# First attention pass as pairs of 64-row products, with one side bank and a new order of the work

## The chip, the cores and the metric

The kernel runs on one core of a Trainium2 chip. The metric is the time of one execution on the device, in microseconds (us). The kernel before was run three times.

## The reference

A stack of six transformer layers (model width 256, 16 heads of 16, hidden width 1024) works on 4 sequences of 512 tokens, and a mixture of experts follows. All is float32 at the interface.

```python
for i in range(6):
    xn = adaln(x, cond, n1_w[i], n1_b[i])            # layer norm, scale and shift from cond
    q, k, v = split(xn @ qkv_w[i].T)                 # rope on q and k, 16 heads of 16
    x = x + softmax(q @ k.T / 4 + mask) @ v @ so_w[i].T
    xn = adaln(x, cond, n2_w[i], n2_b[i])
    # queries from xn, keys and values from ctx (512 rows)
    x = x + softmax(q @ kc.T / 4 + mask2) @ vc @ co_w[i].T
    xn = adaln(x, cond, n3_w[i], n3_b[i])
    x = x + gelu(xn @ f1_w[i].T + f1_b[i]) @ f2_w[i].T + f2_b[i]
# then: layer norm, router over 8 experts, top 2, capacity 640, gelu MLP of width 512
```

The change lies in the six layers. The experts at the end (the last 350 us or so) are not touched.

## The kernel before

**Jobs and slots.** One job is the attention of one sequence in one layer: 8 jobs a layer (4 self, 4 cross), 48 in all. Jobs overlap in a pipeline of slots: slot k runs the first pass of job k, the second pass of job k-1, the tail of job k-2 (normalise, output projection and, for a cross job, the whole feed-forward net) and the head of job k+1 (norm, query and key projections, rope, split into bf16 parts). Slots whose tail is a cross job carry the feed-forward work and are called long here; the others are short. There are 24 short slots with a tail, 24 long ones (two of which, at the end, have no first pass), and slots 0 and 1.

**The two passes.** Scores need float32 accuracy, so q and k are each split in three bf16 parts (high, mid, low), and six products of parts are summed inside one matmul by stacking them over the contraction: 96 rows and a mask row, 97 in all, in `qstack` and `kstack`. The first pass (`pass1`, L735) computes a tile of 128 queries by 512 keys into a ring of three PSUM banks `ps1`, and VectorE takes its row maximum (`maximum`, L949). The maxima are transposed and written as two more rows of `qstack` (chunk M, `shift_rows`). The second pass (`pass2`, L710) computes the transposed tile with the maximum already subtracted, 99 rows, into a ring of two banks `ps2`, and ScalarE takes the exponential (`exp`, L778) into `prob`. The value product (`pv`, L723) is float32 and runs for four heads at once, one in each 32-column strip of the array.

**Units.** A slot has 16 units. A unit has four first-pass tiles, four second-pass tiles, and the value products of the unit before. TensorE executes strictly in this order:

```python
for i in range(TT):                      # four steps of a unit
    if p1: pass1(k, u, i)
    if p2: pass2(k - 1, u, i)
    if i == PV_STEP: pv(k - 1, u - 1)    # PV_STEP = 1
    if i in CHUNK_STEPS: ...side chunks at place 2 * u + (0 or 1)
```

**Side chunks.** Everything else on TensorE is cut in chunks of one PSUM bank, placed at 32 places of the slot by a table written by hand (`CHUNK_PLACES`): HV, HQ, HK are projections for values, queries and keys; HT, T1, T2, LT are transposes; O is the output projection; F1 and F2 the feed-forward net; M the maxima. They go through two banks `side[0]` and `side[1]` in turn. A chunk may start when the chunk two before it has been read (`begin`). Readers: VectorE for T1, HQ, HK, O, F2; ScalarE for HT, LT, T2, HV, M and F1 (the Gelu, two of 256 columns a chunk).

**Other engines.** ScalarE and VectorE run their own copies of the same order, so what stands ahead of an exponential or a maximum delays it. ScalarE also copies the value products out (`copy_group`, L786, once in four units), makes the high and mid bf16 parts (`hi`, `mid`, L818 and L822) and loads the Gelu table and then the exponential table again in each half of the feed-forward net. GpSimd does the rope sums and the residuals of the split (L573 to L578). SyncE's queue writes the parts to DRAM (one DMA for queries, one for keys) and loads the stacks of the next job (13 DMAs for each half of the heads), in order, with its waits in the same queue.

Of the kernel before, what the change touches and what calls it, by code (L numbers as in the profile page):

```python
# [26 lines left out]
B, S = 4, 512  # L27
T = B * S
NE, FE, CAP = 8, 512, 640
P = 128  # L30
# [23 lines left out]


NORM_STEPS = {
    "HT": dict(stats=[0, 1, 2, 3], aggregate=4, newton=6, tiles=[6, 7, 8, 8]),
    "LT": dict(stats=[30, 31, 32, 33], aggregate=34, newton=35, tiles=[35, 35, 35, 35]),
}
GUESS_PLACES = {"HT": 2, "LT": 18}  # L60

SPLIT_PLACES = (10, 12, 16, 18)

PV_STEP = 1
LAST_COPY_STEP = 2
# [3 lines left out]
Q_PARTS = (0, 0, 0, 1, 1, 2)  # L69
K_PARTS = (0, 1, 2, 0, 1, 0)  # L70
NPROD = len(Q_PARTS)
MASK_ROW = NPROD * HD
SHIFT_ROW = MASK_ROW + 1
ROWS = SHIFT_ROW + 2
VROW = H * (HD + 1) + HD
FT = DFF // P
CHUNKS_PER_LAYER = 192
# [19 lines left out]
def is_cross(k):  # L97
    return k % NJ >= B

# [180 lines left out]
def layers(nc, a, x, mod, ident, identb, eps, maskrow, rows, acc, s_pad):  # L280
    with ExitStack() as ctx:
# [9 lines left out]
        qs = [sb(f"qstack{i}", [ROWS, H, S], BF16) for i in range(2)]  # L291
        ks = [sb(f"kstack{i}", [ROWS, H, S], BF16) for i in range(2)]
        parts = sb("parts", [P, 3, KD, S], BF16)
# [3 lines left out]
        v = [sb(f"v{b}", [P, TT, VROW]) for b in range(B)]  # L297
        xnT = sb("xnT", [P, KD, S])
        xnat = sb("xnat", [P, TT, D])
# [3 lines left out]
        hT = sb("hT", [P, FT, S // 2])  # L303

        aT = hT[:, 0:4, :].rearrange("p (k a) n -> p k (a n)", k=KD)
# [6 lines left out]
        mpart = sb("mpart", [P, 2, TT, 2, H // 2], BF16)  # L312
# [9 lines left out]
        bounce = [nc.dram_tensor(f"bounce{i}", (3, D, S), BF16, kind="Internal").ap() for i in range(2)]  # L322
# [14 lines left out]
        s_stack = [sem(f"stack_loaded{i}") for i in range(2)]  # L337
# [12 lines left out]
        s_read = [sem(f"chunk_read{i}") for i in range(2)]  # L350
# [14 lines left out]
        STACK_DMAS = 16 * (2 * NPROD + 1)  # L365

        def slot_chunks(k):
# [3 lines left out]
            ffn = tail and is_cross(k - 2)  # L371
# [5 lines left out]
            def put(*names):  # L377
                for name in names:
                    for c, at in enumerate(CHUNK_PLACES[name]):
                        plan[at].append((name, c))  # L380
# [3 lines left out]
            if p2:  # L384
                plan[SHIFT_PLACES[1]].append(("M", 1))
            if head:
                put("HT", "HQ", "HK")
            if ffn:
                put("LT")
            if p1:  # L390
                plan[SHIFT_PLACES[0]].append(("M", 0))
                put("HV")
            if ffn:
                for th in range(2):
                    plan[FFN1_PLACES[th]] += [("F1", c) for c in range(4 * th, 4 * th + 4)]
                    plan[FFN2_PLACES[th]].append(("F2", th))
# [14 lines left out]
        def wait_read(eng, place, k, what, c):  # L411
            n = number[(k, what, c)]
            eng.wait_ge(s_read[n % 2], place.at(n // 2 + 1, CHUNKS_PER_LAYER // 2))

        def bank_of(k, what, c):
            n = number[(k, what, c)]
            return side[:, n % 2, :], s_read[n % 2]
# [4 lines left out]

        def slot_of(j, n, ring):

            return (n + (j % NJ if ring == 3 else 0)) % ring

        def back_of(j, n, ring):

            return (n - 2 if j % NJ or n > 1 else n - 1) if ring == 3 else n - 1
# [18 lines left out]
        def _(sp):  # L448
# [20 lines left out]
            def shift_rows(k, j, hf):  # L469

                wait_read(sp, place, k, "M", hf)
                for r in range(2):
                    sp.dma_start(qs[j % 2][SHIFT_ROW + r:SHIFT_ROW + r + 1, 8 * hf:8 * hf + 8, :],
                                 mrow[8 * r:8 * r + 8, hf, :]).then_inc(s_mload[hf], 16)

            def write_parts(j):
                for w in range(2):
                    if j > 0 and w == 0:

                        for hf in range(2):  # L480
                            sp.wait_ge(s_stack[hf], place.jobs(j, STACK_DMAS))

                    sp.wait_ge(s_low, place.jobs(j, 2) + w + 1)
                    sp.dma_start(bounce[w].rearrange("r (t p) n -> p (r t) n", p=P),
                                 parts[:, :, :, :].rearrange("p r t n -> p (r t) n")).then_inc(s_bounce[w], 16)

            def load_stack(j, hf):
                if hf == 0:
                    for w in range(2):
                        sp.wait_ge(s_bounce[w], place.jobs(j + 1, 16))  # L490
# [3 lines left out]
                heads = slice(8 * hf, 8 * hf + 8)  # L494
                for w, (stack, order) in enumerate(((qs, Q_PARTS), (ks, K_PARTS))):
                    for r, part in enumerate(order):
# [16 lines left out]
            def slot(k, p2, p1, tail, head):  # L513
# [16 lines left out]
                if k == 0:  # L530

                    sp.wait_ge(s_init, 4)
# [5 lines left out]
                if head:  # L538
                    load_stack(k + 1, 1)
# [953 lines left out]
```

## Time and profile before

| | |
|---|---|
| median of three runs | 4598.32 us (4593.73 to 4600.26) |
| profiled execution, its own time | 4588.98 us |
| its span, first to last instruction | 4587.2 us |
| mean granted TensorE clock | 0.955 of full speed |
| TensorE matmul busy | 4168.8 us (91%) |
| VectorE busy | 2848.2 us (62%) |
| ScalarE busy | 2599.2 us (57%) |
| GpSimd busy | 828.0 us (18%) |

The matmul rows overlap, since matmuls are pipelined: one of 512 columns has a row of about 0.39 us, and the next can start 0.22 us after it. So the distance between starts tells TensorE's pace, and the busy share does not. The layers run from about 110 us to 4262 us of the span.

### The profile page before, as it was taken

Reading aid. Unit: us, or ns where it says so; the run is one execution under the profiler, and the core shown is the slowest. Engines: PE = TensorE matmul, PEld = TensorE weight load, DVE = VectorE, ACT = ScalarE, POOL = GpSimd, SP = SyncE. Lnnn points to the kernel's source line nnn. Section 1 sums busy time; section 2 is a strip of 40 time slices with the busy share of each in tenths; the row PEclk is TensorE's granted clock in tenths of the full one; section 3 lists DMA queues with packets and bytes.
Section 4 is the critical chain, followed back from the end, with each engine's and each line's share of the span. In section 5 each row is a group of like instructions: output and inputs, shape, how many; then the busy total and the mean of one; then the engine's idle time right before and its main releaser. Section 6 shows DMA issues by size and latency. Waiting matters only on the chain. (4 is left out here: it accounts for less than half of the span.)

```text
span 4587.2 us, 71696 instructions
## 1 busy us (share of the span) xinstructions
PE 4168.8 (91%) x20630; PEld 2034.7 (44%) x20630; DVE 2848.2 (62%) x5817; ACT 2599.2 (57%) x4638; POOL 828.0 (18%) x506
## 2 busy tenths in 40 slices
PE   2899999999999999999999999999999999998467
PEld 1243355543355543355543355543445543355445
DVE  3878755577755577855567855567765577851311
ACT  1466655556655556655556655556655566665212
POOL 3211211111211112211112211112211112200033
PEclk7899999999999999999999999999999999999789
DMA  5444422245332244332244332244423244320234
GB/s 151 75 97 87 84 43 43 43 91 90 79 51 43 43 91 85 79 56 43 43 91 80 77 60 46 43 90 75 82 53 53 43 101 85 80 47 12 73 98 97
DMA packets 179055, 321.11 MB, mean 70 GB/s; under 512 B 27928, under 2 KB 144288, under 8 KB 159904
## 3 DMA queue, kind: packets, MB, share of 16 engines
q1 hardware_dynamic: 171360, 306.69, 33.5%
q0 software_dynamic: 7296, 9.51, 1.2%
q8 instruction: 201, 3.29, 0.3%
q14 instruction: 198, 1.62, 0.2%
HBM read 226.63 MB, written 95.17 MB: 70 GB/s over the span
## 5 line engine op out<-in xcount | busy, mean ns | idle before, releaser
L949 DVE TENSOR_REDUCE negmax<-ps 128x1 f32<-128x512 f32 x3072 | 1979.1, 682 | 759.5 <-PE ps L735 738.9
L778 ACT ACTIVATE prob<-ps 128x512 f32<-128x512 f32 x3072 | 1718.5, 595 | 1156.1 <-PE ps L710 1123.3
L735 PE MATMUL ps<-kstack,qstack 97*128 97x512 bf16 x3072 | 1201.7, 392 | 108.2 <-DMA kstack<-maskrow 56.5
L710 PE MATMUL ps<-qstack,kstack 99*128 99x512 bf16 x3072 | 1194.8, 389 | 83.0 <-ACT prob L778 65.0
L723 PE MATMUL psv<-prob,v 128*32 128x512 f32 x6144 | 837.8, 618 | 0.7 <-ACT prob L778 0.7
L735 PEld LDWEIGHTS ps<-kstack,qstack 97*128 97x128 bf16 x3072 | 300.5, 98 | 1004.5 <-DVE negmax L949 598.6
L573 POOL TENSOR_TENSOR rot<-ropep 128x512 f32<-128x512 f32 x96 | 122.0, 1271 | 2627.5 <-DVE ropep L981 2598.0
L710 PEld LDWEIGHTS ps<-qstack,kstack 99*128 99x128 bf16 x3072 | 301.8, 98 | 645.1 <-ACT prob L778 457.5
L987 DVE TENSOR_TENSOR x<-x,side 128x512 f32<-128x512 f32 x144 | 99.0, 687 | 475.6 <-PE side L630 475.6
L689 PE MATMUL side<-anat,wf 128*128 128x256 f32 x1536 | 343.8, 382 | 1.0 <-ACT anat L808 0.9
L630 PE MATMUL side<-wf,hT 128*128 128x256 f32 x1536 | 340.3, 380 | 1.9 <-issue 1.9
L630 PEld LDWEIGHTS side<-wf,hT 128*128 128x128 f32 x1536 | 292.3, 190 | 46.9 <-issue 2.7
L689 PEld LDWEIGHTS side<-anat,wf 128*128 128x128 f32 x1536 | 290.6, 191 | 45.2 <-issue 5.6
L578 POOL TENSOR_TENSOR parts<-rot,parts 128x1024 bf16<-128x1024 f32 x96 | 204.1, 2126 | 324.0 <-ACT parts L822 324.0
L576 POOL TENSOR_TENSOR rot<-rot,parts 128x1024 f32<-128x1024 f32 x96 | 204.8, 2133 | 272.8 <-ACT parts L818 272.8
L723 PEld LDWEIGHTS psv<-prob,v 128*32 128x32 f32 x6144 | 121.9, 109 | 264.8 <-issue 188.5
L850 ACT ACTIVATE hT<-side,f1b 128x256 f32<-128x256 f32 x384 | 160.9, 470 | 131.5 <-PE side L689 130.9
L622 PE MATMUL side<-xnT,wself 128*128 128x512 f32 x384 | 182.8, 600 | 1.1 <-ACT xnT L808 0.9
L616 PE MATMUL side<-ident,xnat 128*128 128x128 f32 x576 | 106.2, 316 | 67.8 <-DVE xnat L941 67.8
L941 DVE TENSOR_SCALAR xnat<-x,mv,y 128x256 f32<-128x256 f32 x288 | 153.1, 566 | 2.6
L980 DVE TENSOR_TENSOR ropep<-side,cos 128x512 f32<-128x512 f32 x96 | 66.4, 692 | 116.6 <-PE side L622 113.9
L786 ACT ACTIVATE osum<-psv 128x512 f32<-128x512 f32 x192 | 114.4, 596 | 41.9 <-PE psv L723 41.9
(154 smaller groups left out, 3486.2 us busy)
## 6 DMA issues: line engine op xcount, KB each, us to landing
bounce<-parts SPq DMA_DIRECT2D x96, 768.0 KB, 3.7
qstack<-bounce SPq DMA_DIRECT2D x576, 128.0 KB
kstack<-bounce SPq DMA_DIRECT2D x576, 128.0 KB
ctxT<-in_ctxT SPq DMA_DIRECT2D x24, 512.0 KB, 5.5
nw<-in_nwT SPq DMA_DIRECT2D x18, 512.0 KB, 11.3
w<-in_w SPq DMA_DIRECT2D x16, 512.0 KB, 4.9
wself<-in_wself SPq DMA_DIRECT2D x24, 256.0 KB, 5.0
wcross<-in_wcross SPq DMA_DIRECT2D x24, 256.0 KB, 4.2
```

What stands on the lines that cost most here:

```text
L576: nc.gpsimd.tensor_tensor(rot[:, :, :], rot[:, :, :], parts[:, 0, :, :], ALU.subtract).then_inc(s_r1, 1)
L578: nc.gpsimd.tensor_tensor(parts[:, 2, :, :], rot[:, :, :], parts[:, 1, :, :], ALU.subtract).then_inc(s_low, 1)
L622: mm = nc.tensor.matmul(bank, w[:, k, m * P:(m + 1) * P], act_T[:, k, :], start=(k == 0), stop=(k == KD - 1))
L630: mm = nc.tensor.matmul(bank[:, i * D:(i + 1) * D], act_T[:, k, t * P:(t + 1) * P], w[:, k, :], start=(k == 0), stop=(k == nk - 1))
L689: mm = nc.tensor.matmul(bank[:, i * D:(i + 1) * D], wf1[:, kk, f * P:(f + 1) * P], nT[:, kk, th * (S // 2):(th + 1) * (S // 2)], start=(kk ...
L710: nc.tensor.matmul(ps2[:, slot_of(j, n, RING2), :], kk[:, h, kt * P:(kt + 1) * P], q[:, h, :], start=True, stop=True).then_inc(s_p2full, 1)
L723: mm = nc.tensor.matmul(psv[32 * i:32 * i + 32, 0, :], v[j % B][:, kt, (HD + 1) * h:(HD + 1) * h + 32], prob[:, 4 * (u % 2) + i, :], start ...
L735: nc.tensor.matmul(ps1[:, slot_of(j, n, RING1), :], q[0:SHIFT_ROW, h, t * P:(t + 1) * P], kk[0:SHIFT_ROW, h, :], start=True, stop=True).th ...
L778: nc.scalar.activation(prob[:, 4 * (u % 2) + i, :], ps2[:, slot_of(j, n, RING2), :], ACT.Exp, scale=HD ** -0.5).then_inc(s_prob, 1)
L850: ins = nc.scalar.activation(hT[:, f, :], bank[:, i * D:(i + 1) * D], ACT.Gelu, bias=f1b[:, f:f + 1])
L941: ins = nc.vector.tensor_scalar(xnat[:, t, :], x[:, TT * (j % B) + t, :], mv[:, t, 0:1], y0[:, t:t + 1], ALU.subtract, ALU.mult)
L949: nc.vector.tensor_reduce(negmax[:, h // 8, t, h % 8:h % 8 + 1], ps1[:, slot_of(j, n, RING1), :], AX, ALU.max, negate=True).then_inc(s_p1f ...
```

## The change

1. The six part products are split in two blocks of three (48 rows each). A first-pass product now contracts 49 rows (three of the part products and the mask), and heads h and h+8 have theirs in different halves of the partitions, so that the two run on two 64-row tiles of the array at once, into two banks. The first pass is 32 pairs in place of 64 products, and one VectorE instruction takes the maxima of two banks.
2. `ps1` has four banks (two pairs). The side chunks have one bank in place of two.
3. The order of a unit is written anew: one second-pass product, two pairs of the first pass, the value products, second-pass product, side chunk, second-pass product, side chunk, second-pass product.
4. F1 is read by VectorE (bias only), and Gelu is one ScalarE instruction of 2048 columns over SBUF for each half. F2 is four chunks, not two. Long and short slots have their own tables of places.
5. Each of the twelve blocks of parts is written to DRAM by its own DMA, and the stacks are loaded by 10 DMAs for each half of the heads.

```diff
-RING1 = 3
 RING2 = 2
-CHUNK_STEPS = (0, 2)
-CHUNK_PLACES = {
-    "HV": [1, 3], "T1": [4, 5, 6, 7], "HT": [5, 6], "HQ": [7, 8], "HK": [10, 11],
-    "T2": [11, 12], "O": [13, 14], "LT": [19, 20],
+PAIRS = 32
+SHORT_PLACES = {
+    "HV": [1, 3], "T1": [2, 4, 5, 7], "HT": [6, 8], "HQ": [9, 10], "HK": [12, 14],
+    "T2": [15, 17], "O": [19, 21],
 }
-SHIFT_PLACES = (20, 4)
-FFN1_PLACES = (22, 28)
-FFN2_PLACES = (25, 31)
+LONG_PLACES = {
+    "HV": [1, 3], "T1": [2, 4, 5, 7], "HT": [6, 8], "T2": [9, 10], "O": [11, 12], "HQ": [13, 14],
+    "HK": [15, 16], "LT": [17, 18], "F1": [19, 20, 21, 22, 23, 24, 25, 26], "F2": [27, 28, 30, 31],
 }
+SHORT_SHIFT, LONG_SHIFT = (23, 0), (29, 0)
...
-SPLIT_PLACES = (10, 12, 16, 18)
+SHORT_SPLIT = (13, 15, 18, 20)
+LONG_SPLIT = (16, 18, 20, 22)
+GELU_PLACES = (23, 27)
...
-Q_PARTS = (0, 0, 0, 1, 1, 2)
-K_PARTS = (0, 1, 2, 0, 1, 0)
+Q_PARTS = (0, 0, 1, 0, 1, 2)
+K_PARTS = (0, 1, 0, 2, 1, 0)
...
-        ps1 = psum("ps1", RING1)
+        ps1 = psum("ps1", 4)
...
-        side = psum("side", 2)
+        side = psum("side", 1)
...
             def begin(k, what, c):
                 n = number[(k, what, c)]
-                if n >= 2:
-                    pe.wait_ge(s_read[n % 2], place.at(n // 2, CHUNKS_PER_LAYER // 2))
-                return side[:, n % 2, :]
+                if n >= 1:
+                    pe.wait_ge(s_read, place.at(n, CHUNKS_PER_LAYER))
+                return side[:, 0, :]
...
+            def pass1(j, n):
+                m, t = divmod(n, TT)
+                if n % 16 == 0:
+                    pe.wait_ge(s_first[n // 16], place.jobs(j + 1, FIRST_DMAS))
+                if j > 0 or n >= 2:
+                    pe.wait_ge(s_p1free, place.jobs(j, PAIRS) + n - 1)
+                for e in range(2):
+                    rows = slice(first_rows(e), first_rows(e) + FIRST_ROWS)
+                    mm = nc.tensor.matmul(ps1[:, 2 * (n % 2) + e, :], qs[j % 2][rows, 8 * e + m, t * P:(t + 1) * P],
+                                          ks[j % 2][rows, 8 * e + m, :], start=True, stop=True)
+                mm.then_inc(s_p1full, 1)
...
             def slot(k, p2, p1, tail, head):
                 for u in range(SLOT_UNITS):
...
+                    if p2:
+                        pass2(k - 1, u, 0)
+                    if p1:
+                        pass1(k, 2 * u)
+                        pass1(k, 2 * u + 1)
+                    if u and p2:
+                        pv(k - 1, u - 1)
...
+                    if p2:
+                        pass2(k - 1, u, 1)
+                    for what, c in plan[2 * u]:
+                        side_work(k, what, c)
+                    if p2:
+                        pass2(k - 1, u, 2)
+                    for what, c in plan[2 * u + 1]:
+                        side_work(k, what, c)
+                    if p2:
+                        pass2(k - 1, u, 3)
...
+            def gelu(k, th):
+                wait_read(act, place, k, "F1", 4 * th + 3)
+                nc.scalar.activation(hT[th][:, :, :], hT[th][:, :, :], ACT.Gelu).then_inc(s_gelu, 1)
+                act.preload_act_table_set(EXP_SET)
...
# ScalarE, in each half unit: exponentials 0 and 1 (or 2), copy_group, side chunk, guess, hi or mid, gelu, then exponential 3
+                    if p2:
+                        for i in ((0, 1), (2,))[half]:
                             exp(k - 1, u, i)
...
+                    if ffn and at in GELU_PLACES:
+                        gelu(k, GELU_PLACES.index(at))
+                    if half == 1 and p2:
+                        exp(k - 1, u, 3)
...
# VectorE, in each half unit: one maximum of two banks, side chunk, steps of the norm
-                nc.vector.tensor_reduce(negmax[:, h // 8, t, h % 8:h % 8 + 1], ps1[:, slot_of(j, n, RING1), :], AX, ALU.max,
+                nc.vector.tensor_reduce(out_at, ps1[:, 2 * (n % 2):2 * (n % 2) + 2, :], AX, ALU.max,
                                         negate=True).then_inc(s_p1free, 1)
...
+                elif what == "F1":
+                    th, cc = divmod(c, 4)
+                    for i in range(2):
+                        f = 2 * cc + i
+                        ins = nc.vector.tensor_scalar(hT[th][:, f, :], bank[:, i * D:(i + 1) * D], f1b[:, f:f + 1], None, ALU.add)
+                    ins.then_inc(s_read, 1)
```

## Rows read from the trace of the kernel before

**Rows 1.** The page: busy time, share of the span, instructions.

```profile
span 4587.2 us, 71696 instructions
PE 4168.8 (91%) x20630; PEld 2034.7 (44%) x20630; DVE 2848.2 (62%) x5817; ACT 2599.2 (57%) x4638; POOL 828.0 (18%) x506
```

**Rows 2.** Groups by line: xcount, busy us, mean ns, idle before and releasers.

```profile
L949 DVE TENSOR_REDUCE negmax<-ps 128x1 f32<-128x512 f32 x3072 | 1979.1, 682 | 759.5 <-PE ps L735 738.9 <-issue 14.2
L778 ACT ACTIVATE prob<-ps 128x512 f32<-128x512 f32 x3072 | 1718.5, 595 | 1156.1 <-PE ps L710 1123.3 <-issue 5.2 <-PE psv L723 4.8
L818 ACT ACTIVATE parts<-rot 128x1024 bf16<-128x1024 f32 x96 | 101.0, 1052 | 49.5 <-POOL rot L574 36.7 <-DMA bounce<-parts 12.8
...
L968 DVE TENSOR_TENSOR anat<-side,recip 128x256 f32<-128x256 f32 x192 | 81.4, 424 | 6.6
L808 ACT ACTIVATE xnT<-side,mod 128x512 f32<-128x512 f32 x96 | 74.6, 777 | 38.5 <-PE side L616 37.2
L980 DVE TENSOR_TENSOR ropep<-side,cos 128x512 f32<-128x512 f32 x96 | 66.4, 692 | 116.6 <-PE side L622 113.9 <-POOL rot L574 2.7
L850 ACT ACT_TABLE_LOAD x48 | 61.6, 1283 | 0.8
```

**Rows 3.** Windows of three short and two long slots; the last pair is DMA.

```profile
core 0: us, PE busy (x) PEld busy (x) DVE busy (x) ACT busy (x) POOL busy (x), PEclk, DMA share, GB/s
1134.05:1201.78 67.73, 66.21 (x345) 26.39 (x345) 53.95 (x108) 46.26 (x84) 13.51 (x8) 1.00 0.44 79
1826.28:1893.81 67.53, 66.30 (x346) 26.37 (x345) 53.79 (x107) 46.20 (x84) 13.52 (x8) 1.00 0.45 80
3829.01:3895.70 66.69, 65.87 (x344) 25.77 (x344) 52.16 (x102) 44.70 (x81) 13.50 (x8) 1.00 0.44 89
1305.22:1410.01 104.79, 98.71 (x482) 52.62 (x480) 61.98 (x125) 60.02 (x106) 15.87 (x9) 0.95 0.26 47
...
3381.34:3485.73 104.39, 99.03 (x482) 52.66 (x481) 61.95 (x125) 60.02 (x106) 15.86 (x9) 0.95 0.26 47
```

**Rows 4.** Timeline (start, us, what, idle before): a unit without side chunks.

```profile
1173.26 1.06 PE L723 MATMUL psv<-prob,v 128*32 128x512 f32 x8
1174.26 0.39 PE L735 MATMUL ps<-kstack,qstack 97*128 97x512 bf16 x1
1174.48 0.38 PE L710 MATMUL ps<-qstack,kstack 99*128 99x512 bf16 x1
1174.68 2.48 DVE L949 TENSOR_REDUCE negmax<-ps 128x1 f32<-128x512 f32 x4 [0.47 <-PE ps L735]
...
1174.90 1.76 ACT L778 ACTIVATE prob<-ps 128x512 f32<-128x512 f32 x3 [0.94 <-PE ps L710]
...
1176.04 0.10 PEld L710 LDWEIGHTS ps<-qstack,kstack 99*128 99x128 bf16 x1 [0.31 <-ACT prob L778]
1176.04 0.39 PE L710 MATMUL ps<-qstack,kstack 99*128 99x512 bf16 x1
1176.36 1.07 PE L723 MATMUL psv<-prob,v 128*32 128x512 f32 x8
```

**Rows 5.** Timeline of a unit with a value chunk, then ScalarE reading it.

```profile
2000.62 1.89 PE L630 MATMUL side<-wcross,ctxT 128*128 128x256 f32 x8
2002.35 0.38 PE L735 MATMUL ps<-kstack,qstack 97*128 97x512 bf16 x1
2002.55 0.60 ACT L836 ACTIVATE v<-side 128x512 f32<-128x512 f32 x1 [0.64 <-PE side L630]
2003.04 1.08 ACT L778 ACTIVATE prob<-ps 128x512 f32<-128x512 f32 x2
```

**Rows 6.** Timeline: VectorE reading a T1 chunk; later a T1 and HT chunk.

```profile
2009.77 0.24 DVE L967 RECIPROCAL recip<-side 128x16 f32<-128x16 f32 x1
2010.05 0.42 DVE L968 TENSOR_TENSOR anat<-side,recip 128x256 f32<-128x256 f32 x1
...
2010.89 0.60 PE L616 MATMUL side<-ident,osum 128*128 128x128 f32 x4
2011.33 0.60 PE L616 MATMUL side<-ident,xnat 128*128 128x128 f32 x4
```

**Rows 7.** Timeline of the slot without a first pass: TensorE and ScalarE.

```profile
4216.04 0.60 PE L710 MATMUL ps<-qstack,kstack 99*128 99x512 bf16 x2
4217.11 0.39 PE L710 MATMUL ps<-qstack,kstack 99*128 99x512 bf16 x1 [0.47 <-ACT prob L778]
4217.43 1.06 PE L723 MATMUL psv<-prob,v 128*32 128x512 f32 x8
4218.43 0.60 PE L710 MATMUL ps<-qstack,kstack 99*128 99x512 bf16 x2
```

**Rows 8.** Timeline of the feed-forward burst in a long slot.

```profile
2057.35 7.17 PE L689 MATMUL side<-anat,wf 128*128 128x256 f32 x32
...
2064.55 0.84 ACT L850 ACTIVATE hT<-side,f1b 128x256 f32<-128x256 f32 x2 [0.89 <-PE side L689]
...
2065.41 1.28 ACT L853 ACT_TABLE_LOAD   x1
```

**Rows 9.** Windows: the slot without second pass; 10 us of the one without first.

```profile
110.31:168.48 58.17, 43.69 (x109) 15.51 (x109) 48.20 (x95) 7.95 (x11) 13.46 (x8) 0.71 0.48 83
4183.00:4193.00 10.00, 7.33 (x43) 2.06 (x42) 4.51 (x18) 6.80 (x14) 1.07 (x1) 1.00 0.01 2
```

**Rows 10.** The page, DMA issues; then SyncE's queue in the timeline.

```profile
bounce<-parts SPq DMA_DIRECT2D x96, 768.0 KB, 3.7
...
2056.36 2.73 SPq L497 DMA_DIRECT2D kstack<-bounce  x6
```

More of the change, by code:

```diff
@@ L378, in put @@
                 for name in names:
-                    for c, at in enumerate(CHUNK_PLACES[name]):
+                    for c, at in enumerate(places[name]):
                         plan[at].append((name, c))
@@ L471, in shift_rows @@
                 wait_read(sp, place, k, "M", hf)
[L472 to L490, printed above, removed]
+                for e in range(2):
+                    at = second_rows(e) + BLOCK
+                    heads = slice(8 * e + 4 * hf, 8 * e + 4 * hf + 4)
+                    sp.dma_start(qs[j % 2][at:at + 2, heads, :], mrow[8 * e:8 * e + 8, hf, :]).then_inc(s_mload[hf], 16)
+            def write_part(j, w, part):
+                order = (Q_PARTS, K_PARTS)[w]
+                if part == 0 and w == 0 and j > 0:
+                    for hf in range(2):
+                        sp.wait_ge(s_first[hf], place.jobs(j, FIRST_DMAS))
+                        sp.wait_ge(s_second[hf], place.jobs(j, SECOND_DMAS))
+                sp.wait_ge((s_hi, s_mid, s_low)[part], place.jobs(j, 2) + w + 1)
+                for r in range(NPROD):
+                    if order[r] == part:
+                        src = low if part == 2 else parts[w][:, part, :, :]
+                        sp.dma_start(bounce[w][r].rearrange("(t p) n -> p t n", p=P), src[:, :, :]).then_inc(s_bounce[w], 16)
@@ new lines, in load_second, with write_and_load @@
+            def load_second(j, hf):
+                for e in range(2):
+                    at = second_rows(e)
+                    heads = slice(8 * e + 4 * hf, 8 * e + 4 * hf + 4)
+                    for w, stack in enumerate((qs, ks)):
+                        sp.dma_start(stack[j % 2][at:at + BLOCK, heads, :],
+                                     bounce[w][NPROD // 2:NPROD].rearrange("r (c h) n -> (r c) h n", h=H)[:, heads, :]).then_inc(s_second[hf], 16)
+            def write_and_load(j):
+                for part in range(3):
+                    write_part(j, 0, part)
+                write_part(j, 1, 0)
+                write_part(j, 1, 1)
+                write_part(j, 1, 2)
+                for w in range(2):
+                    sp.wait_ge(s_bounce[w], place.jobs(j + 1, PART_DMAS))
+                load_first(j, 0)
+                load_second(j, 0)
@@ L797, in modulate @@
                 wait_filled(act, place, k, what, c)
-                bank, read = bank_of(k, what, c)
                 row, b = norm_row(k, what)
@@ new lines, in slot @@
+                    for what, c in plan[at]:
+                        side_work(k, what, c)
+                    if head and at == GUESS_PLACES["HT"]:
+                        rstd_guess(k, "HT")
+                    if ffn and at == GUESS_PLACES["LT"]:
+                        rstd_guess(k, "LT")
+                    if head and at in splits:
+                        step, n = divmod(splits.index(at), 2)[::-1]
+                        (hi, mid)[step](k + 1, n)
+                    if ffn and at in GELU_PLACES:
+                        gelu(k, GELU_PLACES.index(at))
@@ L984, in side_work @@
                     t0 = TT * (j % B) + 2 * c
-                    if what == "F2" and c == 0:
-                        dve.wait_ge(s_bias, place.at(cross_before(j) + 1, B))
                     nc.vector.tensor_tensor(x[:, t0:t0 + 2, :], x[:, t0:t0 + 2, :], bank.rearrange("p (t d) -> p t d", t=2),
-                                            ALU.add).then_inc(read, 1)
+                                            ALU.add).then_inc(s_read, 1)
             def head0():
@@ new lines, in slot @@
+                ffn = is_ffn(k)
+                for at in range(2 * SLOT_UNITS):
+                    u, half = divmod(at, 2)
+                    if p1:
+                        maximum(k, at)
+                        if at == 17:
+                            shift_parts(k, 0)
+                    for what, c in plan[at]:
+                        side_work(k, what, c)
+                    for what, wanted in (("HT", head), ("LT", ffn)):
+                        places = NORM_PLACES[what]
+                        if not wanted:
+                            continue
+                        for t in range(TT):
+                            if at == places["stats"][t]:
+                                stats(k, what, t)
+                        if at == places["aggregate"]:
+                            aggregate(what)
+                        if at == places["newton"]:
+                            normalise(k, what)
+                        for t in range(TT):
+                            if at == places["tiles"][t]:
+                                normed(k, what, t)
```

324 lines of the change are left out of this document (139 added, 185 removed).

## The prediction

> **What bounds the kernel now.** I read the page first: TensorE's rows cover 91% of the span, VectorE's 62%, ScalarE's 57% [rows 1]. The groups by line agree: the maxima and the exponentials both sat idle mostly until a score product came, 739 and 1123 us of it [rows 2]. So TensorE is the nearest bound. The windows by slot then show two kinds: short slots of 66.7 to 67.7 us with TensorE at full clock, and long ones of 104.4 to 104.8 us at clock 0.95 [rows 3]. Chunk paces: HV, HQ, HK, O (two each) 1.73 [rows 5], T1, T2, HT (eight) 0.44 [rows 6], M about 0.4: 18 us of side work in a short slot; with LT, F1 and F2 (0.9 and 13.8 each) 46.5 in a long one. ScalarE is busy for 45 of 67 and 60 of 105 us there, VectorE for 53 and 62.
>
> The timeline gives the pace. A 512-column bf16 product is followed by the next 0.22 us later. From a second-pass product to the value products it is 0.31, from their start to the next product 1.00 [rows 4]; the other products stand at 0.22, so entering the column-tiled form costs 0.09 more. From value products to value products a unit without side work takes 3.10 us. Its pure TensorE pace is 8 x 0.22 + 0.09 + 1.00 = 2.85, so 0.25 is stall, and the rows name it: second-pass products wait for the exponential two before (0.31 idle on the weight load of 1176.04). That loop can be read alone in the slot without a first pass: products at 4216.04 and 0.22 later, the third at 4217.11, so 1.07 us from a product to the one that reuses its bank [rows 7]: 0.42 until the exponential starts, 0.6 for it, 0.06 for the release [rows 4]. Exponentials back to back are 0.48 apart [rows 5].
>
> **The first pass.** Per unit four products at 0.22 (0.88) become two pairs at 0.22 (0.44), if the two halves of a pair really run together. The trace has no row-tiled product; the nearest is the value product, where four column tiles start together and four 512-column float32 products of two rows each take 1.00, not four times that [rows 4]. Ends: 0.22 a pair (together) and 0.44 (one after the other, no gain). I take 0.22. One more change of tile form stands in each unit (full, row, column, full in place of full, column, full): 0.09. Gain: 0.35 a unit, 5.6 us a slot, 270 us over 48 jobs, if nothing waits. The Trainium skill ("TensorEngine Tiling (Array Packing)", Key Properties) says that a change of mode drains the engine; the 0.09 agrees. Its section PSUM Bottleneck says that tiling speeds up the products and not the emptying of PSUM; that rule speaks against this change, and the working below is what it comes to here.
>
> **VectorE.** A maximum over two banks: above 0.68 (one of today's) and below 1.37 (two) [rows 2]. Today's follow each other at 0.60 (four in 2.48) [rows 4], so near 1.2; 2.4 a unit, under every unit time below. No term.
>
> **The order of a unit.** Today second-pass products are spread over the unit, so that ScalarE works while TensorE does first-pass products and side chunks. Now products 1, 2, 3 and the next unit's 0 follow each other, and between 3 and the value products stand only product 0 and two pairs: 0.22 + 0.31 + 0.22 + 0.31 = 1.06, just the 1.07 that exponential 3 needs. Whatever delays exponential 3 now stalls TensorE. From product 3 to the next unit's product 1 is 1.06 + 1.00, some 2.04 (I use 0.98 for the last step). A unit without chunks, product 1 at 0: product 2 at 0.22, product 3 waits for exponential 1 until 1.06, product 0 for exponential 2 until 1.55, the pairs at 1.86 and 2.08, value products at 2.39, the next product 1 at 3.37. Pure pace is 2.48, so 0.89 is stall, and the unit is 0.27 longer than today's 3.10. A check from the trace: with no first pass at all, value products to value products are still 0.31 + 0.22 + 1.07 + 1.00 and more, some 2.8 to 3.3 [rows 7].
>
> **One side bank.** A chunk of pace X is followed by its reader 0.20 after X (2000.62 + 1.73, reader at 2002.55) [rows 5]. Readers: 0.60 for a ScalarE copy [rows 5], 0.78 for HT and LT, two VectorE products (0.60 + 0.69) for HQ and HK, one such for O [rows 2], 0.70 for T1 [rows 6], two of 256 columns, 0.76, for F1 by the 0.42 of such a row [rows 2]. Then 0.07 to release. Between the two places of one unit stands one product (0.22). So the second chunk stalls by 0.20 + reader + 0.07 - 0.22: 0.6 (ScalarE) to 1.3 (HQ, HK). Today two banks hide all of it: in the feed-forward burst four chunks run at their pace of 1.73, 32 rows in 7.17 us [rows 8]. Further, a ScalarE reader in the second place stands ahead of exponential 3, and copy_group (0.60), hi and mid (1.05 [rows 2]) stand ahead of exponential 2 or 3.
>
> **Short slot, unit by unit**, by these steps (us): 0 (M, HV, copy) 6.1; 1 (T1, HV) 5.7; 2 (T1, T1) 4.1; 3 (HT, T1) 4.2; 4 (HT, HQ, copy) 6.0; 5 (HQ) 4.8; 6 (HK, hi) 5.4; 7 (HK, T2, mid) 7.2; 8 (T2, copy) 4.0; 9 (hi, O) 4.3; 10 (mid, O) 4.3; 11 (M) 3.5; 12 (copy) 3.9; 13 to 15 at 3.37, 10.1. One of them in full, unit 7: HK from 0.22 to 1.94, read by 3.42, T2 starts 3.49, product 3 at 3.95, T2 read from 4.15, mid to 5.6, exponential 3 to 6.17, value products 6.24, next product 1 at 7.22. Sum 73.8, against 67.3 (mean of the three windows [rows 3]): +6.5. All of the gain of 5.6 is gone, and 12 of stall are added. Over 24 short slots: +156.
>
> **Long slot.** Chunks at all 32 places. Units: 6.1, 5.7, 4.1, 4.2, 5.0, 5.3, 6.7, 7.3, 7.9 (VectorE is late with the norm behind HK), 5.5, 6.8, 9.0, 6.8, 9.1, 7.0, 9.9: 106.2. In units 11 and 13 stands the new Gelu: today ScalarE's Gelu is hidden under the burst (it waits 0.89 before each chunk [rows 8]); now table load 1.28, Gelu of 2048 columns, table load 1.28 stand ahead of exponential 3. The trace has 1024 columns at 1.05 and 512 at 0.60 [rows 2], so 2.0 by the same slope (between 1.05 and 3.8, eight times the 0.47 of a 256-column one): 4.5 in all. TensorE has 2.8 of work beside it in unit 11 and more in unit 13, so the two cost 2.3 and 0.6 beyond what a pair of chunks costs. Low clock, as today 0.95, is worth some 2 us. 108 against 104.6: take +4, times 22: +88. The two slots at the end without a first pass: chunks wait singly for their reads, and two Gelus stand bare, about +15 together; slots 0 and 1 cancel (in slot 0 VectorE sets the pace and gains 3).
>
> **Queues.** SyncE issues 12 + 20 + 4 DMAs a slot, not 2 + 26 + 4, at 0.46 us [rows 10]: hidden. The stack's last block in a short slot: mid ends in unit 10 at about 2.0, GpSimd 2.1, bounce 3.7 (its landing now [rows 10]), ten loads 4.6, the M rows 1 and landing 3: 16.4; the slot ends 21 us after unit 10 begins. Cover 5 us; if it were gone, each us over it would be paid 24 times. Bytes written to DRAM double, at a DMA share of 0.44 [rows 3].
>
> **Sum.** 4589 (profiled execution) + 156 + 88 + 15 = 4848; the median of the runs shown is 9 above the profiled execution. Forecast 4850.
>
> **Rivals.** (a) Faster: today's stalls stay what they are (4 us in a short slot, some 12 in a long one, 67.3 and 104.6 less 16 x 2.85 and the side work) and the 5.6 us a slot come through: 4589 - 270 = 4319. For it: the first pass is TensorE time in every slot. Against: the read of the one bank has no cover in some 10 units of a short slot, and exponential 3 has no slack. It decides when the added stall is under 5.6 a slot; half of my 12 would give 4590. (b) The pairs don't run together, or the weights of the second pair aren't loaded behind the first: the value products of today load all eight weights ahead (a form that overlaps), but on other tiles. Price 0.44 a unit on the path, 7 a slot, +335: about 5180. The Trainium skill ("TensorE: Matmul & The Clock Gate", Part 3) says that a weight load overlaps running products only in another row group; by that the second pair would cost about 0.1 to 0.2 more a unit, and the sum would be 4930 to 5000; no row here shows it. (c) The clock: the slot with a first pass alone had VectorE as its pace and clock 0.71 [rows 9]. The slot without a first pass, whose products also wait for exponentials, kept full clock [rows 9], so I give little; a clock of 0.9 in short slots would add some 6 a slot, 150: 5000. (d) Gain and loss cancel: 4580 to 4610.
>
> **How the numbers follow.** Forecast 0.66, (a) 0.17, (b) 0.08, (c) 0.05, (d) 0.04. Range of the likeliest alone 4720 to 4980: a third of the reckoned stall either way. With part of (a), (c) and (d) it is 4550 to 5040. A change of 0.2% (9 us) is about what can be told. Faster 0.17, same 0.03, slower 0.80.
>
> **What would show it.** Right: in short slots TensorE starts of the two halves of a pair a few ns apart and pairs 0.22 apart; units without chunks near 3.4; the second of two chunks in a unit starting 0.6 to 1.3 after product 2, its weight load released by the reader; value products waiting for L778; 9 us in units 11 and 13 of long slots. Wrong: short slots under 67 us (then (a)), a pair at 0.44 (b), clock under 0.95 in short slots (c), or waits on stack DMAs at slot starts.

## The result and the profile after

The changed kernel takes 5070.8 us (5065.0 to 5079.7), the kernel before 4596.0 in the same session: ratio 1.104, 95% interval 1.102 to 1.105. Its profiled execution has a span of 5078.0 us, 491 more than before. The sign was forecast, the size was not: 4850 was said, and the top of the range was 5040.

The page of the changed kernel: span, busy shares, and the groups that answer to [rows 1, 2].

```profile
span 5078.0 us, 68492 instructions
PE 4048.6 (80%) x20630; PEld 1852.5 (36%) x20630; DVE 2903.2 (57%) x4711; ACT 2525.8 (50%) x4302; POOL 856.6 (17%) x518
...
L837 ACT ACTIVATE prob<-ps 128x512 f32<-128x512 f32 x3072 | 1741.4, 595 | 1810.0 <-PE ps L761 1787.4
L1001 DVE TENSOR_REDUCE negmax<-ps 128x2 f32<-128x1024 f32 x1536 | 1839.2, 1222 | 387.6 <-PE ps L788 366.7
...
L788 PE MATMUL ps<-kstack,qstack 49*128 49x512 bf16 x3072 | 498.2, 391 | 115.1 <-DVE negmax L1001 94.1
```

The row of L788 shows that the row tiles work: 3072 products of 0.39 us each cover 498 us, where one at a time they covered 1202. The two halves of a pair start 3 or 4 ns apart, and the second pair 0.22 us after the first wherever it has nothing to wait for. No engine is fuller than before. The exponentials sat idle for 1810 us, 654 more than in [rows 2], waiting for a second-pass product, and the weight loads of those products in turn waited for exponentials. Two engines wait for each other in turn: what sets the pace is a chain of latencies, not a full engine.

Windows of two short slots and two long ones, from second-pass product 0 to the next slot's; they answer to [rows 3].

```profile
2642.00:2721.00 79.00, 64.78 (x345) 22.87 (x345) 52.75 (x74) 45.47 (x83) 13.57 (x8) 0.98 0.36 88
3409.84:3488.87 79.03, 64.80 (x345) 22.89 (x345) 52.79 (x74) 45.48 (x83) 13.56 (x8) 0.98 0.37 88
2106.08:2217.07 110.99, 92.90 (x480) 47.13 (x481) 63.33 (x109) 57.02 (x92) 15.82 (x9) 0.98 0.30 72
2217.07:2330.80 113.73, 95.86 (x481) 48.39 (x480) 63.72 (x111) 57.08 (x92) 15.82 (x9) 0.95 0.24 57
```

The same distances averaged over all slots account for the span. Short slots: 18 at 78.3 (67.8 before) and the first of each layer, 6, at 79.7 (72.2). Long slots: 21 at 113.2 (103.8), and slot 47, which has no next job to prepare, at 99.4 (90.6). That is 189 + 45 + 206 = 440. The first two slots with what precedes them add 20, and what follows slot 47, with its Gelus bare, 31.

A unit without chunks in the timeline of the changed kernel; it answers to [rows 4].

```profile
2020.27 0.61 PE L761 MATMUL ps<-qstack,kstack 114*128 114x512 bf16 x2
2020.70 2.25 ACT L837 ACTIVATE prob<-ps 128x512 f32<-128x512 f32 x4 [1.18 <-PE ps L761]
2021.35 0.88 PE L761 MATMUL ps<-qstack,kstack 114*128 114x512 bf16 x2 [0.47 <-ACT prob L837]
2021.84 0.10 PEld L761 LDWEIGHTS ps<-qstack,kstack 114*128 114x128 bf16 x1 [0.39 <-ACT prob L837]
2022.16 0.61 PE L788 MATMUL ps<-kstack,qstack 49*128 49x512 bf16 x4
2022.70 1.07 PE L774 MATMUL psv<-prob,v 128*32 128x512 f32 x8
2023.69 0.11 PEld L761 LDWEIGHTS ps<-qstack,kstack 114*128 114x128 bf16 x2 [0.84 <-ACT prob L837]
```

In words: products 1 and 2 at 2020.27 and 0.22 later, product 3 at 2021.35 (1.08 after product 1: the loop of [rows 7]), product 0 at 2021.84, the two pairs at 2022.16 in 0.54, value products at 2022.70, the next product 1 at 2023.69: 3.42 us. The forecast for this unit was 3.37, and 3.10 before.

### The profile page after: what moved, and what is told of

Same layout as the page of the kernel before. It is cut to its first block and busy times, and to the rows that moved or that the text cites. A ratio compares the mean times of both kernels' runs of the same rounds, so it can differ in the third digit from the quotient of the medians.

```text
span 5078.0 us, 68492 instructions
## 1 busy us (share of the span) xinstructions
PE 4048.6 (80%) x20630; PEld 1852.5 (36%) x20630; DVE 2903.2 (57%) x4711; ACT 2525.8 (50%) x4302; POOL 856.6 (17%) x518
## 3 DMA queue, kind: packets, MB, share of 16 engines
q8 instruction: 196, 3.21, 0.3%
q14 instruction: 183, 1.49, 0.1%
## 5 line engine op out<-in xcount | busy, mean ns | idle before, releaser
L1001 DVE TENSOR_REDUCE negmax<-ps 128x2 f32<-128x1024 f32 x1536 | 1839.2, 1222 | 387.6 <-PE ps L788 366.7
L761 PE MATMUL ps<-qstack,kstack 114*128 114x512 bf16 x3072 | 1076.6, 392 | 136.2 <-ACT prob L837 120.4
L761 PEld LDWEIGHTS ps<-qstack,kstack 114*128 114x128 bf16 x3072 | 283.6, 98 | 1118.4 <-ACT prob L837 809.2
L788 PE MATMUL ps<-kstack,qstack 49*128 49x512 bf16 x3072 | 498.2, 391 | 115.1 <-DVE negmax L1001 94.1
L736 PE MATMUL side<-anat,wf 128*128 128x256 f32 x1536 | 397.8, 404 | 82.2 <-DVE hT L1039 58.6
L1039 DVE TENSOR_SCALAR hT<-side,f1b 128x256 f32<-128x256 f32 x384 | 168.2, 480 | 477.7 <-PE side L736 477.7
L625 POOL TENSOR_TENSOR low<-rot,parts 128x1024 bf16<-128x1024 f32 x96 | 204.5, 2130 | 482.1 <-ACT parts L876 482.1
L788 PEld LDWEIGHTS ps<-kstack,qstack 49*128 49x128 bf16 x3072 | 101.9, 94 | 440.3 <-issue 288.7
L663 PE MATMUL side<-ident,osum 128*128 128x128 f32 x768 | 120.8, 279 | 70.7 <-ACT xnT L866 39.7
L663 PE MATMUL side<-ident,hT 128*128 128x128 f32 x576 | 99.2, 300 | 87.3 <-DVE hT L991 85.6
```

The source lines that it names most:

```text
L625: nc.gpsimd.tensor_tensor(low[:, :, :], rot[:, :, :], parts[w][:, 1, :, :], ALU.subtract).then_inc(s_low, 1)
L663: tr = nc.tensor.transpose(bank[:, i * P:(i + 1) * P], tile, ident[:, :])
L736: mm = nc.tensor.matmul(bank[:, i * D:(i + 1) * D], wf1[:, kk, f * P:(f + 1) * P], nT[:, kk, th * (S // 2):(th + 1) * (S // 2)], start=(kk ...
L761: nc.tensor.matmul(ps2[:, n % RING2, :], kk[0:ROWS, h, kt * P:(kt + 1) * P], q[0:ROWS, h, :], start=True, stop=True).then_inc(s_p2full, 1)
L788: mm = nc.tensor.matmul(ps1[:, 2 * (n % 2) + e, :], qs[j % 2][rows, 8 * e + m, t * P:(t + 1) * P], ks[j % 2][rows, 8 * e + m, :], start=Tr ...
L1001: nc.vector.tensor_reduce(out_at, ps1[:, 2 * (n % 2):2 * (n % 2) + 2, :], AX, ALU.max, negate=True).then_inc(s_p1free, 1)
```

## The experiments

Short and long in what follows are the mean distances from product 0 to product 0 in each run's own trace, the first short slot of a layer and slot 47 left out; a unit's time is the median over these slots. Units are numbered as in the prediction and run from product 1 to product 1 (from product 0 to product 0 in the kernel before and in the orders in which a product of the first pass comes first). The diffs are cut to what matters. Each ratio is to the kernel before in the same session, whose median moved between 4586 and 4596 us; differences between runs are of their times as they stand.

**Maxima first.**

```diff
 if p1:
-    maximum(k, at)
+    if half == 0:
+        maximum(k, at)
+        maximum(k, at + 1)
```

> The changed kernel with one edit: VectorE takes both maxima of a unit before it reads the unit's side chunks. Theory A (what the sum of the prediction lacked is mostly VectorE's order: the second maximum stands behind the read of the first place's chunk, so the next unit's second pair waits): the waits before the second pair of units 3, 6 and 7, 2.8 us a short slot and 0.8 a long one, go; part may come back as waits for exponential 3. About 5070 - 24 x 2.8 - 22 x 0.8 = 4985, between 4960 and 5020. Rival B (those waits only stand where another would): 5060 to 5080.

Measured 4993.1, ratio to the kernel before 1.087 (1.084 to 1.089): 78 us less than the change, as theory A said. Short slots went from 78.3 to 75.2 us. Long ones gained nothing (113.2 to 113.5), where theory A had 0.8 each: their second pair of unit 3 stopped waiting (0.54 us), but units 8 to 12 grew by 0.7 together. The timeline of the changed kernel shows the wait that went, in units 5 and 6 of a short slot:

```profile
1981.14 0.69 DVE L1033 TENSOR_TENSOR ropep<-side,sin 128x512 f32<-128x512 f32 x1 [1.49 <-PE side L669]
1981.75 0.68 DVE L1034 TENSOR_TENSOR ropep<-side,cos 128x512 f32<-128x512 f32 x1
1982.33 0.39 PE L788 MATMUL ps<-kstack,qstack 49*128 49x512 bf16 x2
1982.35 2.35 DVE L1001 TENSOR_REDUCE negmax<-ps 128x2 f32<-128x1024 f32 x2
1983.62 0.39 PE L788 MATMUL ps<-kstack,qstack 49*128 49x512 bf16 x2 [0.90 <-DVE negmax L1001]
```

VectorE sat idle for 1.49 us before 1981.14, waiting for the HQ chunk, while a maximum that it could have taken stood behind that read in its order. It took it at 1982.35, and the second pair, 0.22 after the first by pace, came 1.29 after it. With the maxima first, the same place in the other trace reads:

```profile
1952.02 0.69 DVE L1033 TENSOR_TENSOR ropep<-side,sin 128x512 f32<-128x512 f32 x1 [0.36 <-PE side L669]
1952.23 1.76 ACT L837 ACTIVATE prob<-ps 128x512 f32<-128x512 f32 x3 [1.34 <-PE ps L761]
1952.62 0.68 DVE L1034 TENSOR_TENSOR ropep<-side,cos 128x512 f32<-128x512 f32 x1
1952.88 0.39 PE L761 MATMUL ps<-qstack,kstack 114*128 114x512 bf16 x1 [0.47 <-ACT prob L837]
1953.21 0.60 PE L788 MATMUL ps<-kstack,qstack 49*128 49x512 bf16 x4
```

All four products go in 0.60. The granted clock of short slots rose from 0.98 to 1.00 as well, so a part of the 78 us is clock. Of the 3.1 us a short slot, 2.4 were gained in units 2, 5 and 6, whose next unit's second pair had waited, and 0.7 in units 7 and 8, where no pair had waited and the clock had been at half in 10 of the 18 slots.

**One side bank in the old kernel.**

```diff
-    if n >= 2: pe.wait_ge(s_read[n % 2], ...n // 2...)
-    return side[:, n % 2, :]
+    if n >= 1: pe.wait_ge(s_read[(n - 1) % 2], ...(n - 1) // 2 + 1...)
+    return side[:, 0, :]
```

> The kernel before, with one side bank in place of two and nothing else. Theory A (an uncovered read costs 0.20 + reader + 0.07): no cover where chunks share a place (T1 beside HT, HK beside T2, the four F1), little after HQ: some 4 us a short slot, 12 a long one: 4596 + 24 x 4 + 24 x 12 = 4980, between 4850 and 5080. Rival B (the bank is not what costs, the order of the second pass is): under 4700.

Measured 5255.2, ratio 1.145 (1.142 to 1.147). More than theory A said (5080 at most) and far from B. Short slots 76.4, long ones 123.0 (19 more; units 11 and 14, each with four F1 chunks at one place, took 14.5 against 10.9 and 10.6). In a table of places made for two banks, where up to four chunks stand together, the second bank is worth 660 us. The changed kernel has tables of its own, with one chunk a place; with them and the old order of the unit one bank costs nothing on balance (the next run).

**The old order around the pairs.**

```diff
-P2(0), pair, pair, PV, P2(1), chunk, P2(2), chunk, P2(3)
+pair, P2(0), chunk, P2(1), PV, pair, P2(2), chunk, P2(3)
```

(In words. P2 is a product of the second pass, PV the value products. ScalarE's order follows: exponential 0, chunk, 1, copy, 2, chunk, 3.)

> The changed kernel (pairs on row tiles, one side bank, its own tables of places, Gelu over SBUF) with the unit in the order of the kernel before: pair, second-pass product 0, chunk, product 1, value products, pair, product 2, chunk, product 3. Theory A (the clustered second pass and the read of the bank without cover are the cost, and this order covers both): pure pace of a unit 2.68, reads covered by 1.8 us after the first place and 0.8 after the second: short slots 66 to 68, long ones 100 to 104, time 4500 to 4640. Rival B (one bank costs about as much in any order): 4850 to 5000. Rival C (the pairs or their form changes cost): unit without chunks over 3.3, time over 4750.

Measured 4576.5, ratio 0.996 (0.995 to 0.997): theory A, and 494 us less than the change with the same pairs, the same single bank, the same tables, Gelu and DMAs. This one edit of TensorE's and ScalarE's order gives back all that was lost. Short 69.7 and long 101.0: short slots missed the expected 66 to 68, because a unit without chunks took 3.21 and not 2.9. That is 0.11 more than the 3.10 of the kernel before, so in this order too the pairs shorten no such unit.

**The new order around single products.**

```diff
-P1, P2(0), chunk, P1, P2(1), PV, P1, P2(2), chunk, P1, P2(3)
+P2(0), P1, P1, PV, P1, P1, P2(1), chunk, P2(2), chunk, P2(3)
```

> The kernel before (97-row products one at a time, ring of three, two side banks, its own places) with second-pass products clustered as in the change: product 0, two first-pass products, value products, two first-pass products, product 1, chunk, product 2, chunk, product 3; VectorE reads chunks after the third and fourth maximum. Theory A (the clustering alone costs): a unit without chunks 3.7 in place of 3.10, units with a ScalarE reader or copy 0.5 to 1 more: short slots 72 to 75, long ones 106 to 110: 4750 to 4880. Rival B (only the bank costs): 4590 to 4650.

Measured 5300.6, ratio 1.154 (1.152 to 1.157). A unit without chunks took 3.75 (3.7 said), but short slots took 81.8 and long ones 119.4, where 72 to 75 and 106 to 110 were said, and the time is 420 us over theory A's range: the units with chunks lost more than I gave them. VectorE's order was changed too in this run (chunks after the third and fourth maximum, the third norm a step later), so the excess of the units with chunks isn't shown to be the cluster's alone; that of the units without chunks is. In its timeline:

```profile
2195.04 0.60 PE L710 MATMUL ps<-qstack,kstack 99*128 99x512 bf16 x2
2195.46 1.68 ACT L787 ACTIVATE prob<-ps 128x512 f32<-128x512 f32 x3 [1.50 <-PE ps L710]
2196.11 0.88 PE L710 MATMUL ps<-qstack,kstack 99*128 99x512 bf16 x2 [0.47 <-ACT prob L787]
2196.82 0.60 PE L735 MATMUL ps<-kstack,qstack 97*128 97x512 bf16 x2
```

ScalarE idles 1.50 before product 1's exponential, and then TensorE idles for ScalarE.

**Both pairs first.** The maxima first, ScalarE's order as in the run with the old order, and:

```diff
+pair, pair, P2(0), chunk, P2(1), PV, P2(2), chunk, P2(3)
```

> The changed kernel with another order of the unit: both pairs, second-pass product 0, chunk, product 1, value products, product 2, chunk, product 3; VectorE takes both maxima first. Theory A (a unit costs its pace as long as 1.07 us lie between a second-pass product and the one that reuses its bank, and the chunk reads are covered): a unit without chunks takes 2.6 (3.21 in the run with the old order, where 0.5 stood before products 0 and 1), short slots 62 to 65, long ones 94 to 98: 4230 to 4380. Rival B (VectorE, with 2.4 us of maxima in 2.6, or the row-tiled pairs side by side become the bound): over 4500.

Measured 4474.3, ratio 0.975 (0.973 to 0.977): between A and B. Short slots 65.5 (62 to 65 said), but long ones 100.5 (94 to 98 said): unit 8 took 11.1 us, VectorE late with the norm. A unit without chunks takes 2.88, not 2.6: I had left out that the exponentials follow each other in a queue (four in 2.24 us), so product 1 waits 0.27 for exponential 3.

**Early norm.** The changed kernel, maxima first, and in long slots:

```diff
+if ffn and at == 15:
+    normalise(k, "LT")
+    for t in range(TT): normed(k, "LT", t)
 for what, c in plan[at]: side_work(k, what, c)
```

> The changed kernel with the maxima first (4993), and in long slots VectorE normalises for the third norm at place 15 ahead of reading HK, not in four steps between the reads of HK. Theory A (what long slots took over my 108 is VectorE being late with the norm behind HK, so that LT waits, 2.9 us in unit 8 and 1 in unit 9): long slots 2 to 3.5 us shorter, 4910 to 4950. Rival B (the excess is the clock and the Gelu): 4975 to 5000.

Measured 4929.3, ratio 1.074 (1.072 to 1.076): 64 us less than with the maxima first, as theory A said. Long slots went from 113.5 to 109.8: units 8 and 9 from 9.7 and 6.6 to 7.9 and 6.0, and units 11 and 12 from 10.0 and 7.7 to 9.2 and 7.0, with the granted clock of long slots up from 0.960 to 0.991. The wait in the changed kernel:

```profile
2268.68 1.54 DVE L991 TENSOR_SCALAR hT<-x,mv,y 128x256 f32<-128x256 f32 x2
...
2270.35 1.11 PE L663 MATMUL side<-ident,hT 128*128 128x128 f32 x4 [2.90 <-DVE hT L991]
...
2273.22 1.93 PE L774 MATMUL psv<-prob,v 128*32 128x512 f32 x8
```

TensorE idles 2.90 us, and then the transposes take 1.11 where [rows 6] have 0.60, the value products 1.93 where they took 1.06: half clock (0.54 granted from 2270 to 2277).

**No Gelu and no tables.**

```diff
-    nc.scalar.activation(hT[th], hT[th], ACT.Gelu)
-    act.preload_act_table_set(EXP_SET)
+    nc.scalar.activation(hT[th], hT[th], ACT.Copy)
```

> As the run with the early norm, but the Gelu is a plain copy of the same 2048 columns and no table is loaded (the Gelu is left out of what is computed). Theory A (tables and Gelu stand bare ahead of exponential 3 in units 11 and 13, 2.6 us of the 4.5 being tables): long slots some 2.5 to 4 us shorter than in that run, clock up, 4830 to 4880. Rival B (the Gelu is covered by the chunks): within 15 us of that run.

Measured 4853.2, ratio 1.057 (1.055 to 1.060): 76 us less, as theory A said. Long slots 106.5, 3.3 less; unit 11 from 9.15 to 6.99, unit 13 from 9.15 to 8.71, so 2.2 and 0.4. The prediction had 2.3 and 0.6 for the whole Gelu there. The copy of 2048 columns is still in place, and unit 11 now takes what unit 12 takes (6.98): beside the chunks the copy costs nothing there, and the table loads are the cost.

**Both pairs first and the early norm together.**

> The order with both pairs first (4474) and the third norm ahead of the reads of HK. Theory A: in that run unit 8 of long slots took 11.1 us because VectorE was late with the norm; with the early norm it is near 7.5, so long slots lose some 4 us: 4474 - 22 x 4 = 4385, between 4360 and 4410. Rival B (another wait takes its place): over 4440.

Measured 4402.1, ratio 0.960 (0.958 to 0.961), 4% faster than the kernel before: theory A, just inside its bound. Long slots 97.4, unit 8 at 8.7 and not 7.5 (7.2 in 9 of the 21 slots). Its unit without chunks, and windows of a short and a long slot:

```profile
1804.75 0.60 PE L761 MATMUL ps<-qstack,kstack 114*128 114x512 bf16 x2
1805.18 1.08 ACT L837 ACTIVATE prob<-ps 128x512 f32<-128x512 f32 x2 [0.64 <-PE ps L761]
1805.29 0.61 PE L788 MATMUL ps<-kstack,qstack 49*128 49x512 bf16 x4
1805.83 0.39 PE L761 MATMUL ps<-qstack,kstack 114*128 114x512 bf16 x1
```

```profile
1680.44:1746.16 65.72, 62.20 (x347) 22.30 (x345) 52.46 (x75) 46.02 (x83) 13.55 (x8) 1.00 0.43 106
1907.97:2004.46 96.49, 91.24 (x482) 46.98 (x481) 64.03 (x111) 57.98 (x93) 15.83 (x9) 1.00 0.28 67
```

From product 2 (1804.75) to product 0 (1805.83), which reuses its bank, are 1.08 us, filled by product 3 and both pairs. In the changed order only product 3 stood between product 2 (2020.49) and product 0 (2021.84).

**Tile 0 twice, then tile 1.**

```diff
-for e in range(2): product(n, e)
+for e in range(2):
+    for nn in (n, n + 1): product(nn, e)
```

(In words; the four also wait together, until the banks of both pairs are read.)

> The changed kernel with the maxima first (4993), the eight products of the first pass in a unit sent as 0a 0b 1a 1b (0 and 1 the row tiles, a and b the pairs), so that the two products of row tile 0 follow each other before those of tile 1 start, 0.22 us more for the four (0.66 for 0.44). Theory A (the first pass lies on the path in most units, between product 0 and the value products): 0.22 x 16 x 48 = 169 us at most; units that wait for exponential 3 hide some of it: 5100 to 5160. Rival B (the first pass is off the path and its shortening could gain nothing): 4990 to 5030. Rival C (the tiles don't run together at all in this form, 0.88): over 5250.

Measured 5035.8, ratio 1.097 (1.096 to 1.099), 43 us more than with the maxima first: between A and B, and it decides nothing, since its premise fell. The products were sent tile 0, tile 0, tile 1, tile 1, but in the trace the first of tile 1 starts 6 or 7 ns after the first of tile 0, and the two others 0.22 later. The first of the four still stood 0.54 before the value products, as in the changed kernel, and a unit without chunks took 3.43 (3.42): nothing was added to TensorE. VectorE got the first pair later (its signal comes at the end of tile 1) and the joint wait came in; which of the two costs the 43 us was not separated.

**Every pair twice.** To put a known amount of first-pass time on TensorE:

```diff
-for e in range(2):
+for e in (0, 1, 0, 1):
```

> The changed kernel with the maxima first (4993), every pair of the first pass sent twice: 0.44 us more TensorE work a unit, the time that the row tiles save against single products. Theory A (the first pass is on the path between product 0 and the value products; in the changed order exponential 3 has just no slack there, so nearly all of it counts): 250 to 340 us more, 5240 to 5330. Rival B (the waits for exponential 3 hide it, so the pairs gained nothing in this order): 4990 to 5060.

Measured 5176.0, ratio 1.127 (1.124 to 1.130): 183 us more, under A's 250 and far over B. A unit without chunks went from 3.42 to 3.85, all of the 0.44; units 6 and 7, where hi and mid stand ahead of exponential 3, stayed at 5.44 and 7.26. Short slots grew by 5.2 us, long ones by 1.6 only, and the clock of the long ones rose from 0.960 to 0.989 with the added work. So the 183 us are what is left after that gain of clock, and not the pure share of the path.

> The kernel with both pairs first and the early norm (4402), every pair sent twice. Theory A (in that order the first pass is TensorE's pace, apart from some 0.3 us a unit in which product 0 or 1 waits for its exponential anyway): 200 to 340 us more, 4600 to 4740, so that without row tiles this order would not beat the kernel before (4590). Rival B (the order alone makes the gain): under 4500.

The same edit in the fastest kernel: 4573.4, ratio 0.995 (0.993 to 0.996), 171 us more and just below A's 200. So with 0.88 us of first pass a unit that order keeps 0.5% of its 4%. Against four single products on the full array the pairs are worth less than these 171 us: in this order they bring two changes of form a unit (0.31 before and behind them in place of 0.22), up to 138 us in all. How much less is open, since no run had single products in this order.

## Why the prediction was right in kind and wrong in size

The time lay 221 us over the forecast and outside the range. By kind of slot, short ones lost 234 us where 156 were reckoned, long ones 206 where 88 were, and the two ends 51 where 15 were. The mechanism was the one described; what failed is the handling of VectorE, once left out and once put too low, and it is named below. Two slips in adding, 73.6 and 106.4 for the units as listed and not 73.8 and 106.2, change little.

*The bound and the pace* (0.22, 0.31, 1.07): right. Units without chunks came out at 3.42 for 3.37, and at 3.75 for 3.7 with single products in the new order. In the two other orders, where two exponentials in a row decide, I was 0.3 short (3.21 for 2.9, 2.88 for 2.6): exponentials in a row are about 0.55 apart (four in 2.25), where the prediction took 0.48.

*The pairs run together*: right. 0.22 a pair, one more change of form at 0.09 (product 0 to pair 0.31 to 0.32). The 0.1 to 0.2 a unit that was set down in rival (b) for the weights of the second pair did not appear: in the unit shown its loads start at 2022.17, right behind the start of the first pair (2022.16), and it follows that pair by 0.22. The kernel before could have told: its products on all rows stood 0.22 apart too, each with a weight load of its own [rows 4]. Rival (b) fell. Doubling the pairs cost 183 us of the possible 338, so the 270 us of my first step were never all there.

*The order of the unit*: right, and it is the cause. The same pairs, bank and tables in the old order took 494 us less, and single products in the new order were slow as well. In units 0, 1, 3, 4 and 8 to 15 of short slots forecast and trace differ by 0.3 at most.

*"VectorE. No term"*: this step failed. I compared the sum of VectorE's work with the unit and not its order. A maximum stands behind a chunk read that waits for TensorE, and the next unit's second pair needs it: 2.8 us in a short slot (0.54, 1.07 and 1.15 before the second pair of units 3, 6 and 7), the difference in units 2, 5 and 6 (4.74, 5.94, 6.04 for 4.1, 4.8, 5.4). With the maxima first these three took 4.20, 4.87 and 5.44. Unit 7, the one worked out in full, took 8.13 for 7.22, at half clock in most slots, and 7.26 with the maxima first. Taking them first gave back 78 us of the 221 by which the forecast was short.

*Long slots*: this is the second term that was put too low, and the larger one. Unit 8 was given 7.9 with VectorE late in it; it took 9.4, TensorE idle for 2.9 of it. Units 9, 11 and 12, partly at half clock, took 6.7, 9.5 and 7.8 for 5.5, 9.0 and 6.8. Normalising earlier gave back 64 us. With both changes short slots are at 75.2 (73.8 said) and long ones at 109.8 (108 said). Of the 79 us that are left over the forecast, some 46 lie in the long slots, 28 at the ends and 6 in the short slots; no run takes them apart further.

*The clock* was given "some 2 us" in long slots and none in short ones. In long slots it stood at 0.964, as in the kernel before. In short ones it fell from 0.992 to 0.982, far from rival (c)'s 0.9, and was 0.999 once the pair no longer waited. It hung on the waits: no run changed it alone, so its share of the 78 and the 64 is not measured by itself (units 7 and 8 put it at some 0.7 us a short slot).

*One side bank*: where it was looked at, a read costs what was said (the T2 chunk of unit 7 was said to start 3.49 after product 1, and did: 1990.98 to 1994.47). Its whole price in the changed kernel stays open, since no run of it had two banks.

*The ends*: 51 us against 15. Nothing was run for the 36; 31 of the 51 come after slot 47.

*Queues*: right. TensorE's products waited for stack loads 25 us in all, 21 of them once, at the first pair; before it was 58, 35 of them once.

## What to carry to other kernels

When an order written by hand is changed, walk the longest loop (product, reader, release, next product in the same bank) through every kind of unit, and then do the same for each reader's own order: an engine with a low busy share that waits in order for one thing holds up all that stands behind it. Put the work that needs nothing from the loop, here the first pass, into the loop's latency, between a product and the one that reuses its bank, and not beside other free work. A saving on the fullest engine is worth its size only where that engine doesn't wait: doubling it on purpose tells how much of it counts.

## What the runs showed of the hardware that was not expected

The granted clock fell to 0.5, the lower of its two levels (1.2 and 2.4 GHz), behind idles of TensorE of 1 to 3 us. All 21 long slots of the changed kernel have the idle of 2.9 us, and in all of them the clock falls during it or behind it; in the run with the early norm, which hasn't that idle, it fell in 10 of 21. Value products behind it took 1.93 us in place of 1.06. In short slots TensorE idled for less each time, 0.90, 0.99, 1.17 and 1.15 us in units 5 to 7, and the clock fell in these units in 10 of 18. A row behind the last of these, and a window after it:

```profile
1997.24 1.94 PE L774 MATMUL psv<-prob,v 128*32 128x512 f32 x8 [1.15 <-ACT prob L837]
```

```profile
1998.00:2001.00 3.00, 3.00 (x15) 1.15 (x7) 2.36 (x4) 1.24 (x3) 2.92 (x3) 0.50 0.66 226
```

With the maxima first the idles of 0.90 and 0.99 are gone, those of 1.17 and 1.15 stay, and the clock fell in 1 short slot of 18. So it was not the last idle alone that brought it down. With the early norm and the maxima first the clock of short slots was 1.00 and of long ones 0.99.

Products on different row tiles don't hold each other up: sent as tile 0, tile 0, tile 1, tile 1, the first product of tile 1 started 6 or 7 ns after the first of tile 0, ahead of the second one of tile 0.

VectorE's normalising rows (256 columns, both operands in SBUF) took a median of 0.40 us in the kernel before where GpSimd ran nothing beside them (245 rows) and 2.34 us where it did (43 rows); in the changed kernel 0.41 (260) and 1.22 (28). The maxima, which read PSUM, show nothing of the kind: their median is 0.68 and 1.22 us with GpSimd at work or without.
